# One-hot counts of a router summed on TensorE instead of VectorE, the causal rows reordered around them, and the last combination shared with TensorE

## What is computed

```
    scores = jnp.where(causal, -jnp.inf, scores)
    weights = jax.nn.softmax(scores, axis=-1)
    return jnp.einsum('nqk,nkd->nqd', weights, V)
...
    loc1 = jnp.take_along_axis(jnp.cumsum(mask1, axis=0), e1[:, None], 1)[:, 0].astype(jnp.int32) - 1
    counts1 = mask1.sum(axis=0)
    loc2 = (jnp.take_along_axis(jnp.cumsum(mask2, axis=0), e2[:, None], 1)[:, 0] + counts1[e2]).astype(jnp.int32) - 1
...
    y = (g1 * v1)[:, None] * yb[idx1] + (g2 * v2)[:, None] * yb[idx2]
```

## Time and profile before

| | |
|---|---|
| median of three runs | 1127.86 us |
| the profiled execution | 1133.31 us, its span 1131.5 us |
| TensorE, VectorE, ScalarE, GpSimd busy in the span | 80%, 66%, 41%, 18% |
| mean granted clock of TensorE | 0.886 of 2.4 GHz |
| causal layer, block 2, rows 0 to 4 | 878.75 to 905.12 us |
| block 3 projected; rows 0 to 4 | 905.12 to 919.85; to 947.2 us |
| first expert tile; last scatter of the experts | 996.69; 1103.41 us |
| last stage | 1105.72 us to the end |

### The profile page before, as it was taken

The page is one execution under the profiler, slowest core; times in us unless marked ns, Lnnn a source line. Parts: engine busy times, 40 slices in busy tenths (PEclk is TensorE's granted clock), DMA queues, the critical chain, the costliest instruction groups (busy, mean ns, idle before and its releaser), DMA issues.

```text
span 1131.5 us, 14851 instructions
## 1 busy us (share of the span) xinstructions
PE 903.7 (80%) x4814; PEld 506.7 (45%) x4815; DVE 742.5 (66%) x1333; ACT 468.0 (41%) x903; POOL 206.8 (18%) x248
## 2 busy tenths in 40 slices
PE   7999979889898898975798289994999796278870
PEld 2323432344323443234565289994567665134430
DVE  4903689998999989999998401113567787712225
ACT  1175249760187602965786133443232431112210
POOL 1000001110011100111000613332000212646550
PEclk9999988896889968895899589998899998689995
DMA  3099526875068740797761366665205002079907
GB/s 108 2 323 270 171 87 170 216 173 148 1 172 214 175 129 0 191 224 175 234 204 83 124 185 196 206 188 204 100 1 205 35 11 89 10 272 400 395 28 273
DMA packets 75406, 180.77 MB, mean 160 GB/s; under 512 B 12155, under 2 KB 48718, under 8 KB 72657
## 3 DMA queue, kind: packets, MB, share of 16 engines
q1 hardware_dynamic: 60944, 143.28, 38.4%
q0 software_dynamic: 14400, 36.71, 14.9%
HBM read 120.05 MB, written 43.69 MB: 145 GB/s over the span
## 4 chain that ended last, share of the span: by engine, by line
PE 36%; DVE 29%; issue 19%; DMA 7%; POOL 5%; ACT 3%; SPq 1%; POOLq 0%; another core or an unknown queue 0%; DVEq 0%; ACTq 0%
DVE hst L1878 10%; PE ps L754 6%; PE ps L1343 5%; DVE mxn L1825 5%; DMA bc<-bc_dram 4%; PE ps L1213 3%; PE ps L1331 2%; PE ps L707 2%; POOL ys_dram L1783 2%; DVE hC L1886 2%; PE ps L1286 2%; PE ps L851 2%; DVE dBu L1867 2%; PE ps L1226 1%; DVE Hs L2452 1%
## 5 line engine op out<-in xcount | busy, mean ns | idle before, releaser
L1825 DVE TENSOR_REDUCE mxn<-ps 128x2 f32<-128x1024 f32 x128 | 150.0, 1219 | 65.9 <-PE ps L754 65.8
L1878 DVE TENSOR_TENSOR_SCAN hst<-dA,dBu 128x1180 f32<-128x1180 f32 x64 | 167.0, 2609 | 3.8 <-PE ps L882 3.2
L1424 ACT ACTIVATE Ph<-ps 128x1024 f32<-128x1024 f32 x128 | 125.1, 1074 | 29.1 <-PE ps L851 25.5
L754 PE MATMUL ps<-Kh,Qh 32*128 32x512 f32 x512 | 115.5, 731 | 11.9 <-DVE mxn L1825 9.3
L851 PE MATMUL ps<-Qh,Kh 32*128 32x512 f32 x512 | 117.3, 719 | 3.9 <-ACT Ph L1424 3.6
L1867 DVE TENSOR_TENSOR dBu<-dtu,bc 128x1180 f32<-128x1180 f32 x64 | 88.2, 1383 | 6.2 <-DMA bc<-bc_dram 4.8
L1762 POOL DMA_DIRECT2D yS<-hC x24 | 20.8, 866 | 380.9 <-DVE hC L1886 380.9
L2181 DVE TENSOR_TENSOR yo<-ps,b2r 128x256 f32<-128x256 f32 x32 | 13.6, 425 | 107.2 <-PE ps L1136 107.2
L1343 PE MATMUL ps<-ring,xgT 128*64 128x256 f32 x512 | 70.0, 395 | 13.4 <-ACT xgT L1716 9.5
L865 PE MATMUL ps<-Ph,Vh 128*32 128x512 f32 x512 | 74.4, 655 | 5.1 <-ACT OT L1428 3.3
L2445 DVE COPY yo<-ps 128x256 f32<-128x256 f32 x64 | 26.7, 423 | 76.9 <-PE ps L1343 62.8
(11 more groups left out here) (270 smaller groups left out, 1493.2 us busy)
## 6 DMA issues: line engine op xcount, KB each, us to landing
ring<-in_we SPq DMA_DIRECT2D x16, 2048.0 KB
bc<-bc_dram SPq DMA_DIRECT2D x48, 590.0 KB, 4.7
W<-in_w SPq DMA_DIRECT2D x46, 512.0 KB, 6.4
yS<-hC POOLq DMA_DIRECT2D x24, 590.0 KB, 6.8
yodd<-hC POOLq DMA_DIRECT2D x24, 590.0 KB, 6.8
xs_dram<-zeros SPq DMA_DIRECT2D x1, 8224.0 KB, 46.0
xg<-xs_dram SPq DMA_DIRECT2D x16, 514.0 KB
ys_dram<-zeros SPq DMA_DIRECT2D x1, 5120.0 KB, 50.6
```

What stands on the lines that cost most here:

```text
L754: m = nc.tensor.matmul(ps[:, banks.start + hh % 2, :], Qh[HR * hh:HR * (hh + 1), hg, P * i:P * (i + 1)], Kh[HR * hh:HR * (hh + 1), hg, :], ...
L1424: nc.scalar.activation(Ph[:, n % 2, 2 * g:2 * g + 2, :], ps[:, turned_banks(b, 2 * n + g), :], ACT.Exp, scale=float(HD) ** -0.5).then_inc( ...
L1825: nc.vector.tensor_reduce(slots32(mxn[:, hg % 2, i, :])[:, 2 * g:2 * g + 2, HD], ps[:, score_banks(b, 2 * u + g), :], AX.X, ALU.max, negat ...
L1878: nc.vector.tensor_tensor_scan(hst[:, k % 2, :, :].rearrange("p c t -> p (c t)"), dA[:, k % 2, :, :].rearrange("p c t -> p (c t)"), dBu[:, ...
```

## The change

`count` is gone from VectorE. In its place `tally` on TensorE multiplies the block's one-hot rows, tile after tile, with an identity (a third matrix in tri5), adds the earlier hsum in the same way, and leaves the sum in PSUM, from which ScalarE copies it to hsum (`tallied`). Around it the rows of the causal layer are reordered, and the forty operations at the end become twenty-four and four additions of what TensorE now makes of the last two tiles of each block, by multiplying the gathered rows with diagonal matrices of the weights. Those matrices are written by VectorE (`diagonals`, four operations after each of the expert groups 3 to 6).

```diff
-        CHOICE_BANK = (3, 7, 2)
-        CHOICE_ROW = (1, 2, 3)
+        CHOICE_BANK = (3, 2, 7)
+        TALLY_BANK = 7
+        DIAG_AT = 3
...
+            def tally(b, bank):
+                pe.wait_ge(dve_hot5, b + 1)
+                dst = ps[:, bank, 0:D]
+                for t in range(NT):
+                    m = nc.tensor.matmul(dst, tri5[:, 2, :], hot5[:, NT * b + t, :, :].rearrange("p k e -> p (k e)"),
+                                         start=(t == 0), stop=(b == 0 and t == NT - 1))
+                if b:
+                    m = nc.tensor.matmul(dst, tri5[:, 2, :], hsum[:, (b - 1) % 2, :, :].rearrange("p k e -> p (k e)"),
+                                         start=False, stop=True)
+                m.then_inc(pe_rank5, 1)
...
                         m.then_inc(pe_pt4, 1)
+                        if i == QT and b >= 2:
+                            pe.wait_ge(dve_h4, NT * b + QT)
+                            rank(b - 2, CHOICE_BANK, 2)
                         if i + 2 < NT:
                             scores(i + 2)
                         elif i == NT - 1 and not last:
                             if b >= 2:
-                                pe.wait_ge(dve_rank5, 3 * (b - 1))
+                                pe.wait_ge(dve_rank5, 3 * (b - 2) + 2)
                             turned(b + 1)
...
-                        if i == 3 and b >= 2:
-                            pe.wait_ge(dve_rank5, 3 * (b - 2) + 2)
...
-                        if b >= 2 and i in CHOICE_ROW:
-                            if i == 2:
-                                pe.wait_ge(dve_h4, NT * b + 2)
-                            part = CHOICE_ROW.index(i)
-                            rank(b - 2, CHOICE_BANK, part)
+                        if b >= 2 and i == 1:
+                            rank(b - 2, CHOICE_BANK, 0)
+                        if b >= 2 and i == 2:
+                            pe.wait_ge(act_p4, NT * b + QT)
+                            rank(b - 2, CHOICE_BANK, 1)
+                        if b >= 2 and i == QT:
+                            pe.wait_ge(dve_rank5, 3 * (b - 1))
+                            tally(b - 2, TALLY_BANK)
...
+                pe.wait_ge(dve_diag5, NB)
+                for b in range(NB):
+                    pe.wait_ge(yg_in[b], 16 + 16)
+                    if b >= 2:
+                        pe.wait_ge(dve_h5, FIN * (b - 1))
+                    for i in range(FT, NT):
+                        at = D * (i - FT)
+                        for k in range(2):
+                            t = nc.tensor.matmul(ps[:, 6 + b % 2, at:at + D], diag5[:, b, i - FT, k, :], yg5[:, b, k, i, :],
+                                                 start=(k == 0), stop=(k == 1))
+                    t.then_inc(pe_y5, 1)
...
+            def tallied(b, bank):
+                act.wait_ge(pe_rank5, 4 * b + 4)
+                nc.scalar.activation(hsum[:, b % 2, :, :].rearrange("p k e -> p (k e)"), ps[:, bank, 0:D], ACT.Copy).then_inc(act_hsum, 1)
...
+                        if b and i >= 2:
+                            turned5(NT * (b - 1) + i - 2, 5)
                         if not last:
                             rows(b + 1, i)
...
-                        if b and i >= 2:
-                            turned5(NT * (b - 1) + i - 2, 5)
-                        if b >= 2 and i == 2:
+                        if b >= 2 and i == 3:
                             sums5(b - 2)
...
-            def count(b):
...
                         if i == 0 and b >= 2:
                             best_two(NT * (b - 1) - 1)
+                        if i == 1 and b >= 2:
                             hots(b - 2)
+                        if i == 2 and b >= 2:
+                            first_rows(b - 2, CHOICE_BANK, 0)
                         if i + 2 < NT:
                             maxima(b, i + 2)
                         if b and i:
                             take_logits(NT * (b - 1) + i - 1, 5 if i - 1 < 3 else 3)
+                        if i >= 3 and b >= 2:
+                            first_rows(b - 2, CHOICE_BANK, i - 2)
...
-                        if b >= 2 and i in CHOICE_ROW:
-                            part = CHOICE_ROW.index(i)
-                            first_rows(b - 2, CHOICE_BANK, part)
-                            if part == 2:
-                                second_rows(b - 2)
-                        if b >= 2 and i == QT:
-                            count(b - 2)
-                        if i and b:
+                        if b == 2 and i == QT:
+                            second_rows(b - 2)
+                        if i and b and not (b == NB - 1 and i == QT):
                             best_two(NT * (b - 1) + i - 1)
...
                 variances(b)
+                second_rows(b - 2)
+                scales5(b)
+                best_two(NT * b - 2)
                 take_logits(NT * b - 1, 3)
                 best_two(NT * b - 1)
-                scales5(b)
                 hots(b - 1)
-                count(b - 1)
...
+                def diagonals(b):
+                    for i in range(FT, NT):
+                        for k in range(2):
+                            d = nc.vector.tensor_scalar(diag5[:, b, i - FT, k, :], ident[:, :], w5[:, NT * b + i, k:k + 1], None, ALU.mult)
+                    d.then_inc(dve_diag5, 1)
...
-                        for t in range(NT * b, NT * (b + 1)):
+                        for t in range(NT * b, NT * b + FT):
...
+                    dve.wait_ge(pe_y5, NP2 + b + 1)
+                    rest = Hs[:, NT * b + FT:NT * (b + 1), :].rearrange("p i d -> p (i d)")
+                    nc.vector.tensor_tensor(rest, rest, ps[:, 6 + b % 2, 0:D * (NT - FT)], ALU.add).then_inc(dve_h5, 1)
```

51 lines of the change are left out of this document (28 added, 23 removed).

## The result

The changed kernel takes 1109.43 us (median of 4 runs, 1107.51 to 1110.99) against 1128.31 us of the kernel before (4 runs): ratio 0.9833, 95% interval 0.9811 to 0.9855, so 18.9 us or 1.7% faster. The prediction was 1112.6 with a range from 1109.5 to 1118.5. The profiled execution of the changed kernel took 1109.72 us, its span is 1107.9.

The account below looks back on a forecast made before the run. TensorE and VectorE wait for each other in the causal blocks, then GpSimd's scatters bound, and VectorE alone the last stage. 0.3 + 3.9 + 5.1 + 2.1 + 1.5 + 2.4 = 15.3 us off 1127.86 gives 1112.6, range 1109.5 to 1118.5.

Parts of the forecast that it names:

- Part 1: Causal block 1: ScalarE makes xaT ahead of xn and xa, saving 0.3 us (bounds 0 and 0.6).
- Part 2: Causal block 2: reordered rows remove waits, the tally costs TensorE time; 3.9 us saved (bounds 2.9 and 5.5).
- (b): Causal block 2: first_rows moved behind the PT copies of rows 3 and 4 frees 3.45 us of TensorE's waits.
- (a): Causal block 2: hots moved behind row 1's PT copy, ScalarE turns xa right after the exponential; 1.1 us saved.
- the tally costs its 0.54: Causal block 2: five bf16 matmuls directly ahead of the next projection cost TensorE their full 0.54 us.
- Parts 3 and 4: Block 3's reordering saves 5.1 us; from row 4 to block 2's choice, shorter VectorE work saves 2.1 and 1.5.
- Part 5: GpSimd's scatters and the experts: chain from the choice on unchanged, sixteen new VectorE operations covered; nothing gained or lost.
- Part 6: Last stage: VectorE's work shared with TensorE saves 2.4 us (bounds 0.8 and 3.6), first block waiting 1.2 for TensorE.
- the first three: Cases covered by the range: forecast with its spread (chance 0.70), half of the reordering (0.12), no last-stage gain (0.08).

Follow-up runs that it names:

- e9: Kernel before, unchanged, profiled on a third chip beside the changed kernel; experts from first tile to last product 102.9 us, no whole time given.
- e10: Changed kernel, unchanged, on the third chip beside the kernel before: ratio 0.9872 (0.9828 to 0.9915).
- e13: Kernel before, unchanged, profiled on a fourth chip beside the changed kernel; experts from first tile to last product 94.03 us, no whole time given.
- e14: Changed kernel, unchanged, on the fourth chip beside the kernel before: 1115.01 us, ratio 0.9888 (0.986 to 0.9916).
- e1: Kernel before, unchanged, profiled and timed once more: 1125.10 us against 1126.04 of the same kernel's other runs, ratio 0.999.
- e5: Changed kernel, unchanged, profiled and timed again on another chip: 1126.51 us against 1138.0 of the kernel before, ratio 0.9895.
- e7: Changed kernel with first_rows of parts 1 and 2 back ahead of the PT copies of rows 3 and 4: ratio 0.9935, 4.2 us slower than the changed kernel.
- e8: Changed kernel with hots back in row 0 and ScalarE's old order of turning xa: 1123.55 us, ratio 0.9888.
- e4: Changed kernel with the counts back on VectorE, no tally on TensorE and no copy on ScalarE: 1112.71 us, ratio 0.9888.
- e12: Changed kernel with 24 more small products on TensorE into an unused bank behind the last rank: 1125.85 us, ratio 0.988.
- e6: Changed kernel with idle bf16 products on TensorE before the first expert tile and before the last stage's gathered rows: 1126.90 us, ratio 0.9917.
- e3: Kernel before with the new last stage alone (diagonals, TensorE's products, VectorE's three tiles and one addition): ratio 0.9987, 1.5 us.
- e15: Changed kernel with four of five tiles of block 0 left to VectorE in the last stage: 1110.09 us, ratio 0.986.
- e11: Changed kernel with each product of the experts made in two halves of 128 columns: 1133.35 us, ratio 0.9955.

## Why the prediction was right or wrong, step by step

The stretches of the profiles of the unchanged programs, in us. All are differences of starts in the timelines; "b1", "b2", "b3" begin with the first transposes of PT in those blocks, "scatter" is the first of block 2. e9 and e10 were taken on one chip, e13 and e14 on another:

| | start to b1 | b1 | b2 | b3 to scatter | to first tile | experts to last product | to first last-stage op | to the end |
|---|---|---|---|---|---|---|---|---|
| before | 843.4 | 35.15 | 41.30 | 43.83 | 33.01 | 103.9 | 11.2 | 19.78 |
| e1 | 849.5 | 35.15 | 41.29 | 44.13 | 32.99 | 94.5 | 10.5 | 19.77 |
| e9 | 846.5 | 35.15 | 41.30 | 43.88 | 33.04 | 102.9 | 12.9 | 19.84 |
| e13 | 846.2 | 35.15 | 42.88 | 44.13 | 33.37 | 94.0 | 10.5 | 19.78 |
| changed | 847.3 | 34.73 | 37.15 | 35.52 | 33.05 | 92.5 | 10.3 | 17.40 |
| e5 | 852.3 | 34.72 | 37.15 | 36.03 | 33.34 | 103.9 | 10.7 | 17.38 |
| e10 | 850.6 | 34.73 | 37.16 | 35.78 | 33.47 | 103.8 | 12.5 | 17.37 |
| e14 | 842.1 | 34.73 | 37.16 | 35.83 | 33.35 | 92.7 | 10.6 | 17.35 |

- Part 1 (0.3): 0.42 measured. Right.
- Part 2 (3.9): 4.15. Right. Undone one by one, (b) is worth 2.7 of its 3.45 in this block (e7) and (a) 1.4 for 1.1 (e8); the tally costs its 0.54 (e4).
- Parts 3 and 4 (5.1 + 2.1 + 1.5 = 8.7): 8.2 by the means of four profiles each (43.99 and 35.79), 8.3 in the first pair, 5.0 of these before row 4's product (5.1 foreseen) and 3.3 behind it (3.6). From row 4's addition to Hs it is 4.53 us to `hots` in place of 6.42 (1.9 less, 2.1 foreseen), and from `hots` 9.14 to the scatter in place of 10.48 (1.3 less, 1.5 foreseen). Right within 0.5, but the 1.3 is luck of the clock. e12 has the same code there, and the windows from `hots` to the first scatter in before, changed and e12 are:

```profile
core 0: us, PE busy (x) PEld busy (x) DVE busy (x) ACT busy (x) POOL busy (x), PEclk, DMA share, GB/s
953.20:963.68 10.48, 9.22 (x56) 7.51 (x56) 8.94 (x31) 5.57 (x19) 0.00 (x0) 0.71 0.09 38
945.54:954.68 9.14, 7.82 (x58) 6.61 (x56) 6.24 (x28) 3.67 (x13) 3.98 (x5) 0.81 0.39 159
948.33:958.73 10.40, 9.21 (x58) 7.58 (x57) 6.25 (x28) 3.68 (x13) 4.00 (x5) 0.67 0.34 136
```

  At a granted clock of 0.67 the same program needs 10.4 us (e6 too), as long as the kernel before at 0.71: there TensorE is the bound (busy 9.21 of 10.40 us), and VectorE, with 6.25 us of work in place of 8.94, only waits longer. Of the nine profiles with this causal code seven take 35.5 to 36.0 us from block 3 to the scatter, e6 and e12 37.1. By all nine parts 3 and 4 are worth 7.9 us.
- Part 5 (nothing): right as to what the programs do. The stretch from the first scatter to the first tile keeps its 33 us (0.2 longer), the diagonals cost nothing, and experts with stops (103.4 and 103.9, means of two) or without (94.3 and 92.6) are alike within 2 us. What is left of the latter's 1.7 us is mostly the first groups: the full clock was granted 6.2 us after the first tile in e1 and 3.2 in the changed kernel, but 3.6 and 6.4 in e9 and e10, the other way round.
- Part 6 (2.4): 2.42. Right in the sum and in each term; e3 has it alone. The granted clock was at half till 1096.7, so in the first two blocks. The Trainium skill's rule ("TensorE: Matmul & The Clock Gate", on the 56 ns gap), by which the first block would not have waited, is not borne out by these fp32 passes: VectorE waited 1.44 us. (That section adds 2.5 ns a matmul at full clock, which the prediction left out; it changes nothing here.)

These stretches sum to 0.42 + 4.15 + 8.2 - 0.2 + 2.42 = 15.0 us, against 15.3. Four comparisons gave 18.8, 11.8, 14.4 and 12.6 us of 1128 (0.9833, 0.9895, 0.9872, 0.9888), 15.1 when weighted by their intervals. That 15.0, 15.1 and 15.3 lie so close is in part luck: part 2 was 0.25 too low and parts 3 and 4 0.5 too high (0.8 with the 7.9 of nine profiles, which makes the sum 14.7), and the comparisons differ by 7 us.

**The step that failed** is not a term but "the range takes the first three: 1109.5 to 1118.5", together with "the runs' median is 5.45 lower, and the same saving gives 1127.86 - 15.3 = 1112.6". The range was built of the cases of the mechanism alone and took a comparison's spread as 2.3 us. Three of the four comparisons (11.8 to 14.4 us saved) would have fallen inside it, the one that was made first did not. The intervals of the first two, 0.9811 to 0.9855 and 0.9867 to 0.9923, don't even touch, so comparisons on different chips differ by more than the interval of one says. The runs show more: one program has single executions from 1119.2 to 1130.3 on one chip, its first 850 us move by up to 10 us from profile to profile, and of the three later intervals of the ratio two don't reach down to 0.9833. So the 3.6 us beyond the sum in the first comparison look like such spread; no part of the change was found that makes them. That is argued, not shown: the timed executions have no traces that would say which stretch held them. One number of the timed runs bears on it, their mean granted clock: in each of the eighteen sets of four or more runs of one program its correlation with the time is negative, the longer runs having the lower clock. It goes from -0.03 to -0.95, and from -0.39 to -0.83 in the six sets of more than ten runs; in e14 the run of 1105.67 us has 0.893, the other five 0.884 to 0.889. The profiles show where this can come from: ahead of block 1 the clock stands at half for 177.5 us in e15 (block 1 starts at 843.1) and for 208.2 us in e5 and e11 (852.3 and 854.8), though over all seventeen profiles the two go together only loosely (0.69). So the clock in the first 850 us may be part of the spread. That is not shown: no run changes it alone, and more waiting may as well be what lowers it.

One lead is left open. On the chips without stops block 1 starts at 846.2 to 851.1 us in three profiles with the old causal code (e1, e3, e13) and at 842.1 to 847.3 in five with the new one, on the chips with stops the other way (843.4 and 846.5 against 843.3 to 854.8 in seven); nothing in the change touches that stretch, and these are too few to tell it from chance. The same three and five profiles also differ in when the experts got the full clock (5.9 to 6.2 us after the first tile against 3.2 to 4.2), and on these chips alone the gain would then be larger than 15.0; but the fourth comparison, on such a chip, gave 12.6. The difference of the two first profiles, 23.6 us, was no measure of the change either: 9.3 of it are what the experts' stage differs by between profiles of the kernel before itself (103.9 and 94.5), and 3.9 in the first 850 us stood against them.

## What to carry to other kernels

Before a difference between two profiles is explained, look at a second profile of the same program: stretches bounded by waits between engines repeated here to 0.01 to 0.6 us (but for block 2 of e13, 1.6 us longer, where the granted clock was at half for 3.4 us, and block 3 of e6 and e12, 1.1 to 1.6 longer, where the clock was lower through the ranks behind row 4), while those with DMA (the first 850 us, the experts) moved by up to 10 us. So judge an edit worth 1 to 3 us by its own stretch, not by the median, which once said -3 us where the stretch said +2.4. Work that waits for an engine's result gains most when it is moved to where its engine waits anyway, behind the copy that others need (e7: 8 us for the place of two calls of one helper).

## What was not expected of the hardware

- On two of the four chips of e1 to e15 TensorE stops some ten times in the experts' stage, mostly for 1.4 to 1.6 us (101.5 to 103.9 us), on two it has two or three waits for gathered rows instead (92.5 to 94.5), with the same programs. Two ideas of the cause were not borne out (e11, e12); none is shown.
- Filling TensorE's idle time with products that need nothing was no help: after 63 of them they came 0.7 us apart in place of 0.11 for 8 us (e6), and the first tile was 2.9 us later.
- After the idle 21 us ahead of the experts the full clock (2.4 GHz) was granted 3.1 to 6.4 us after the first tile, in the same program at either end (3.2 in the changed kernel's first profile, 6.4 in e10), which moves the first group of four pairs between 6.4 and 7.9 us. The clock also moved the same code's stretch from `hots` to the scatter from 9.1 us (0.81 granted) to 10.4 (0.67).
